# The search for a row's 408th smallest value: counts by paired sums and by signs, settling put between the masks, low halves taken from clamped values

## The chip, the cores and the metric

One core of a Trainium2 chip. TensorE (PE, with its weight loads PEld), VectorE (DVE), ScalarE (ACT), GpSimd (POOL) and SyncE (SP, which starts most DMAs) run programs of their own and meet at semaphores. SBUF and PSUM (eight banks of 512 fp32 columns) have 128 partitions. The metric is the device time of one execution of the whole program, in microseconds, as the median of several runs.

## The reference, cut to what matters

The program is a hybrid of two layers with eight stages over 2048 tokens of 128 channels. The change lies in the first one, an attention of 16 heads whose scores are reduced by a running sum FF and pruned:

```
S = relu(att[:, 0]); S[..., 0] = 0; S = S * (1 - eye(T))
FF = cumsum(S shifted down by one row, axis=1)
att = att - FF[:, None]
memory_budget = int(2048 * 0.2)                  # 409
FF_mod = where(causal, FF, inf)
rank = argsort(argsort(FF_mod, axis=-1), axis=-1)
keep = (rank < minimum(memory_budget - 1, i + 1)) | eye(T)   # 408 smallest of each row
att = where(keep, att, -inf);  y = softmax(att) @ v;  y @ w_proj.T + b_proj
```

Instead of sorting, the kernel finds, for each row with more than 408 allowed columns, the value of its 408th smallest FF, and the attention behind it compares with that threshold. FF is never negative, so an fp32's bits order it as an integer does.

## The kernel before, in words

The 2048 rows are 16 tiles of 128; tile t has rows 128t to 128t+127 on the partitions and W = 128(t+1) columns, held as fp32 in `NF[t]`. Tiles 0 to 2 keep everything; tiles 3 to 15 are searched. Before the search, `take_high` (L835) stores the upper 16 bits (sign cleared) of each value in `halves[t]`, as uint16.

The search (L861 to L933) settles the threshold bit by bit, from the top, for all 128 rows of a tile at once: NC = 32 rounds, k = 0 to 31. Rounds 0 to 14 work on the high halves, 16 to 31 on the low ones. In one round, for each of 13 tiles:

- DVE writes a mask in bf16 (L893, L899): 1 where the half lies below the value found so far plus the bit tried. The masks go round seven buffers (`tally`).
- PE adds up the mask (L923): matmuls with an identity `IDB` accumulate pieces of 256 columns into one bank of PSUM, so 256 partial counts remain. Eight banks go round. A piece with 128 columns is left over for even t.
- ACT reads the 256 columns with `accum_out` (L933), which leaves the count in a column of `cnt`. The accumulator is read out by an instruction of its own, which the compiler adds.
- DVE settles: one instruction compares the counts with `lim` (L879), one adds the bit where the count is low enough (L881).

The tiles form two sets, [15, 12, 11, 8, 7, 4, 3] and [14, 13, 10, 9, 6, 5]. A set is settled as a whole behind all masks of the other set: while DVE writes the masks of one set, PE and ACT finish the counts of the other. The order on each engine is that of the loops in the code; no planner is at work in this stage.

Round 15, the sixteenth, is different. DVE counts the values whose high half lies above the one found (L895) and replaces each half by the lower half of the value where the high half matches and by zero elsewhere (L896), one instruction of scalar_tensor_tensor over the whole tile. `lim` is corrected by that count (L875).

At the end DVE joins the halves into `thr` (L906 to L909), and the attention starts (L1195 on): its first matmuls wait for the last count. Its order was planned ahead (`TileOrder`) and does not depend on times at run time. The DMAs that load the keys for it run beside the search, from 98 to about 172 us.

Of the kernel before, what the change touches and what calls it, by code (L numbers as in the profile page):

```python
# [19 lines left out]
KEEP = 408  # L20
# [368 lines left out]
def build(nc, a, out, stages):  # L389
    ctx = ExitStack()  # L390
    with ctx:
# [12 lines left out]
        def reg(at, n):  # L404
            return A[:, at:at + n]
# [163 lines left out]
        def stage1():  # L569
            NF = [reg(D0 + 64 * t * (t + 1), 128 * (t + 1)) for t in range(NT)]  # L570
            AT = D0 + 17408
# [145 lines left out]
            junk = [reg(2048 + 128 * i, 128).bitcast(BF16) for i in range(8)]  # L717
            IDB = SM[:, 400:464].bitcast(BF16)
# [133 lines left out]
            counts = [(k, i, t) for k in range(NC) for i in range(2) for t in sets[i]]  # L852
            count_no = {x: n for n, x in enumerate(counts)}

            def edges(i):
                return place[sets[i][0]], place[sets[i][-1]] + 1

            def settle_no(k, i):
                return 2 * (2 * k + i + 1)

            def search_vector(e, w):  # L861
                for r in (high, low):
                    e.memset(r, 0.0).then_inc(built, 1)
                e.memset(lim, float(KEEP - 1) + 0.5).then_inc(built, 1)
                w.wait_ge(d_const, 16)
                e.tensor_copy(IDB, IDN).then_inc(built, 1)
                w.wait_ge(built, 4)
                w.wait_ge(f_high, 13)
                w.wait_ge(f_summed, upto[15])

                def settle(k, i):
                    lo, hi = edges(i)
                    w.wait_ge(counted, count_no[k, i, sets[i][-1]] + 1)
                    if k == 15:
                        e.tensor_tensor(lim[:, lo:hi], lim[:, lo:hi], cnt[:, lo:hi], ALU.add).then_inc(settled, 2)  # L875
                        return
                    w.wait_ge(settled, settle_no(k, i) - 2)
                    value, bit = (high, 14 - k) if k < 15 else (low, 31 - k)
                    e.tensor_tensor(hit[:, lo:hi], cnt[:, lo:hi], lim[:, lo:hi], ALU.is_le).then_inc(settled, 1)  # L879
                    w.wait_ge(settled, settle_no(k, i) - 1)  # L880
                    e.scalar_tensor_tensor(value[:, lo:hi], hit[:, lo:hi], float(1 << bit), value[:, lo:hi], ALU.mult, ALU.add).then_inc(settled, 1)  # L881

                for k in range(NC):
                    for i in range(2):
                        if k:
                            w.wait_ge(settled, settle_no(k - 1, i))
                        for t in sets[i]:
                            n, s = count_no[k, i, t], place[t]
                            if n >= 7:
                                w.wait_ge(folded, n - 6)  # L890
                            mask = tally[n % 7][:, 0:128 * (t + 1)]
                            if k < 15:
                                e.tensor_scalar(mask, halves[t], high[:, s:s + 1], float(1 << (14 - k)), ALU.subtract, ALU.is_lt).then_inc(masks, 1)  # L893
                            elif k == 15:
                                e.tensor_scalar(mask, halves[t], high[:, s:s + 1], 0.5, ALU.subtract, ALU.is_gt).then_inc(masks, 1)  # L895
                                e.scalar_tensor_tensor(halves[t], halves[t], high[:, s:s + 1], NF[t].bitcast(U16)[:, 0::2], ALU.is_equal, ALU.mult).then_inc(built, 1)  # L896
                            else:
                                w.wait_ge(built, 4 + 13)
                                e.tensor_scalar(mask, halves[t], low[:, s:s + 1], float(1 << (31 - k)), ALU.subtract, ALU.is_lt).then_inc(masks, 1)  # L899
# [4 lines left out]
                settle(NC - 1, 1)  # L904
                w.wait_ge(settled, settle_no(NC - 1, 1))
                e.tensor_scalar(highi, high, 65536.0, None, ALU.mult).then_inc(built, 1)  # L906
                e.tensor_copy(lowi, low).then_inc(built, 1)
                w.wait_ge(built, 4 + 13 + 2)
                e.tensor_tensor(thr.bitcast(I32), highi, lowi, ALU.bitwise_or).then_inc(built, 1)  # L909
                w.wait_ge(built, 4 + 13 + 3)  # L910

            def search_tensor(e, w):
                w.wait_ge(built, 4)
                w.wait_ge(f_relu, upto[15])
                w.wait_ge(f_copied, upto[15])
                for n, (k, i, t) in enumerate(counts):
                    W = 128 * (t + 1)
                    w.wait_ge(masks, n + 1)
                    if n >= 8:
                        w.wait_ge(counted, n - 7)  # L920
                    for c0 in range(0, W, 256):
                        c1 = min(c0 + 256, W)
                        m = e.matmul(bank(n % 8, c1 - c0), IDB, tally[n % 7][:, c0:c1], start=(c0 == 0), stop=(c1 == W))  # L923
                    m.then_inc(folded, 1)

            def search_scalar(e, w):
                w.wait_ge(part, 10)
                for n, (k, i, t) in enumerate(counts):
                    s = place[t]
                    w.wait_ge(folded, n + 1)  # L930
                    if n >= 8:
                        w.wait_ge(counted, n - 7)
                    e.activation(junk[n % 8], bank(n % 8, 256), ACT.Copy, accum_out=cnt[:, s:s + 1]).then_inc(counted, 1)  # L933

# [1937 lines left out]
```

## Time and profile before

| | us |
|---|---|
| median of 3 runs | 2950.25 (2947.14 to 2955.3) |
| the profiled execution | 2931.04 |
| its span | 2929.3 |
| first mask of the search, on DVE | 98.06 |
| last settling ended | 348.3 |
| mean granted TensorE clock | 0.944 of full speed |

The profile shows one execution; its times are from the start of the span. A group's mean is that of one instruction; instructions of one engine can overlap, so starts are often closer together than the durations say. The profiled execution took 19.2 us less than the median of the timed runs.

### The profile page before, as it was taken

How to read it: one execution, taken by the hardware profiler on the slowest of the kernel's cores; microseconds unless marked ns; L12 is line 12 of the kernel's file. 1: busy time of each engine (PE TensorE's matmuls, PEld its weight loads, DVE VectorE, ACT ScalarE, POOL GpSimd, SP SyncE). 2: the span in 40 equal slices, each digit the busy share in tenths (PEclk: the TensorE clock that was granted, in tenths of full speed). 3: DMA queues.
4: the chain of work that ended last, by engine and by line, in shares of the span. 5: the costliest groups of instructions: out<-in, count | busy, mean ns of one | idle time of the engine just before them, and what ended most of it. 6: DMA issues, size and time to landing. Idle time of an engine off the chain costs nothing. (4 is left out here: it accounts for less than half of the span.)

```text
span 2929.3 us, 75687 instructions
## 1 busy us (share of the span) xinstructions
PE 2600.9 (89%) x31004; PEld 1627.1 (56%) x31004; DVE 1844.5 (63%) x5181; ACT 1783.4 (61%) x3488; POOL 345.6 (12%) x718
## 2 busy tenths in 40 slices
PE   8999878888889799999998989999999999896596
PEld 3677756666666452212213546676676767665355
DVE  6999887887886662100002757877777787663862
ACT  3676655565666338999996246666666667531331
POOL 2100142222221010000000100000000000026026
PEclk7998989999999899999998999999999999898598
DMA  3410010111100202100000010000000000303003
GB/s 117 69 27 2 2 17 17 18 17 17 17 11 3 53 1 91 58 19 1 1 1 17 1 40 7 2 7 7 3 7 7 7 2 2 98 14 49 29 15 58
DMA packets 85120, 68.23 MB, mean 23 GB/s; under 512 B 40776, under 2 KB 73688, under 8 KB 84392
## 3 DMA queue, kind: packets, MB, share of 16 engines
q1 hardware_dynamic: 76328, 57.09, 8.3%
q0 software_dynamic: 8448, 6.30, 1.7%
q8 instruction: 247, 4.05, 0.6%
q14 instruction: 97, 0.79, 0.1%
HBM read 47.21 MB, written 19.96 MB: 23 GB/s over the span
## 5 line engine op out<-in xcount | busy, mean ns | idle before, releaser
L1769 ACT ACTIVATE arena<-ps 128x1024 f32<-128x1024 f32 x512 | 474.1, 1282 | 25.9 <-PE ps L1719 24.0
L1220 DVE CUSTOM_DVE_ANT_0 arena<-ps,arena 128x1024 f32<-128x1024 f32 (+7 forms) x384 | 350.0, 931 | 105.0 <-PE ps L1096 88.5
L2147 DVE CUSTOM_DVE_ANT_0 arena<-ps,arena 128x512 f32<-128x512 f32 (+3 forms) x640 | 371.2, 643 | 26.7 <-PE ps L2011 25.8
L1172 ACT ACTIVATE arena<-ps 128x1024 f32<-128x1024 f32 (+3 forms) x320 | 275.0, 896 | 129.1 <-PE ps L1129 125.7
L2104 ACT ACTIVATE arena<-arena 128x1152 f32<-128x1152 f32 (+15 forms) x256 | 306.4, 1199 | 63.2 <-DVE arena L2147 63.2
L2011 PE MATMUL ps<-arena 64*128 64x512 f32 (+3 forms) x1280 | 270.3, 547 | 3.5 <-ACT arena L2080 1.1
L1730 PE MATMUL ps<-arena 128*32 128x512 f32 x2048 | 273.0, 604 | 0.0
L2042 PE MATMUL ps<-arena 128*64 128x128 f32 x4352 | 262.3, 275 | 0.0
L2042 PEld LDWEIGHTS ps<-arena 128*64 128x64 f32 x4352 | 235.3, 137 | 33.4 <-issue 28.7
L923 PE MATMUL ps<-arena 128*128 128x256 bf16 (+1 forms) x2176 | 238.1, 273 | 13.7 <-DVE arena L895 9.2
L2066 ACT COPY arena<-ps 128x512 f32<-128x512 f32 (+3 forms) x410 | 189.6, 517 | 75.8 <-PE ps L2028 73.6
L1860 DVE COPY arena<-ps 128x512 f32<-128x512 f32 x16 | 11.1, 692 | 356.5 <-PE ps L1730 356.5
L1124 PE MATMUL ps<-arena 64*128 64x64 f32 x4352 | 216.2, 231 | 20.3 <-ACT arena L1172 12.2
L923 PEld LDWEIGHTS ps<-arena 128*128 128x128 bf16 x2176 | 207.5, 99 | 44.9 <-DVE arena L895 13.9
L1719 PE MATMUL ps<-arena 64*128 64x512 bf16 (+1 forms) x1152 | 207.2, 442 | 23.0
L1124 PEld LDWEIGHTS ps<-arena 64*128 64x128 f32 x4352 | 192.9, 144 | 57.7 <-ACT arena L1172 29.2
L1719 PEld LDWEIGHTS ps<-arena 64*128 64x128 bf16 (+1 forms) x1152 | 53.3, 113 | 292.7 <-ACT arena L1769 267.1
L933 ACT ACTIVATE arena<-ps 128x256 bf16<-128x256 f32 x416 | 158.0, 383 | 68.4 <-PE ps L923 58.4
L2028 PE MATMUL ps<-arena 64*128 64x64 f32 x4352 | 178.9, 225 | 11.5 <-DVE arena L2162 3.2
L2011 PEld LDWEIGHTS ps<-arena 64*128 64x128 f32 x1280 | 115.8, 186 | 126.4 <-DVE arena L2147 55.7
L2028 PEld LDWEIGHTS ps<-arena 64*128 64x128 f32 x4352 | 160.6, 139 | 35.0 <-ACT arena L2104 11.9
L2068 DVE COPY arena<-ps 128x512 f32<-128x512 f32 (+3 forms) x230 | 136.4, 622 | 68.8 <-PE ps L2028 67.3
(301 smaller groups left out, 4026.4 us busy)
## 6 DMA issues: line engine op xcount, KB each, us to landing
arena<-scr_q SPq DMA_DIRECT2D x256, 32.0 KB
scr_s<-scr_f SPq DMA_DIRECT2D x1, 4096.0 KB, 16.5
arena<-scr_k SPq DMA_DIRECT2D x32, 128.0 KB
arena<-by_head_k SPq DMA_DIRECT2D x16, 192.0 KB
arena<-scr_s SPq DMA_DIRECT2D x16, 192.0 KB, 2.6
arena<-by_head_q SPq DMA_DIRECT2D x28, 96.0 KB
by_head_k<-arena SPq DMA_DIRECT2D x5, 512.0 KB, 4.5
scr_x<-arena SPq DMA_DIRECT2D x2, 1024.0 KB, 5.2
```

What stands on the lines that cost most here:

```text
L923: m = e.matmul(bank(n % 8, c1 - c0), IDB, tally[n % 7][:, c0:c1], start=(c0 == 0), stop=(c1 == W))
L1124: e.matmul(bank(b + half, 64, 64 * (nb * g + x)), scored_block(u, g)[q, at:at + 128], IDN[q, q], is_transpose=True, start=(g == 0 and x == ...
L1172: e.activation(turned_block(u, kc), src, ACT.Exp, scale=-1.0).then_inc(exped, 1)
L1220: e.tensor_tensor_reduce(scored_block(u, g)[:, lo:hi], PS[:, 1024 * (k % 2):1024 * (k % 2) + hi - lo], NF[t][:, lo:hi], -1.0, mxs[:, col - ...
L1719: m = e.matmul(PS[:, at(n) + 512 * i:at(n) + 512 * i + 512], x, y, start=True, stop=True)
L1730: m = e.matmul(PS[32 * g:32 * g + 32, 3072 + 512 * c:3072 + 512 * c + 512], vp4[:, kt, 4 * g + units[u][0], :], PTR[(2 * s[1] + g // 2) % ...
L1769: e.activation(PTR[k % RS], PS[:, at(n):at(n) + 1024], ACT.Sigmoid, scale=float(1 / np.sqrt(8.0))).then_inc(weighed, 1)
L2011: e.matmul(PS[:, base(step) + 512 * g:base(step) + 512 * g + hi - lo], QA[64 * g:64 * g + 64, 128 * t:128 * t + 128], KA[64 * g:64 * g + 6 ...
L2028: m = e.transpose(PS[:, o:o + 64], block[rows, 512 * kc + 128 * b:512 * kc + 128 * b + 128], IDN[rows, rows])
L2042: m = e.matmul(bank(6 + u % 2, 128)[64 * g:64 * g + 64, :], V[:, 1024 * kt + 64 * h:1024 * kt + 64 * h + 64], halves(plan.ring[u, kc])[:, ...
L2104: e.activation(block, block, ACT.Exp, bias=mxs[:, col:col + 1], scale=-1.0, accum_out=sums(u)[:, g:g + 1]).then_inc(exped, 1)
L2147: e.tensor_tensor_reduce(slot(u, t, g)[:, lo:hi], PS[:, base(step) + 512 * g:base(step) + 512 * g + hi - lo], bias, -1.0, mxs[:, col - 1:c ...
```

## The change

All of it lies in the search and its buffers. Nothing behind `thr` is touched.

- Tiles 3, 4, 5 and 6 get no mask and no matmul. ACT counts them by itself: the Sign of (edge - half) over the tile with `accum_out`, written into a scratch buffer. `edge` is a column that DVE prepares after each settling (`next_edge`).
- The tiles 15 and 8, 12 and 11, 14 and 9, 13 and 10 are summed in pairs into one bank. The mask of the first is multiplied by an identity scaled by 2048 (`IDP`), and ACT reads the bank with Identity and a bias column of 32768, whose 256 additions put the unit of the fp32 sum at one. Both counts then lie in the bits of one number. DVE takes the lower one out (`unpack`) before it compares. Tile 7 has a bank of its own. So there are nine masks, five sums and four signs a round, where there were thirteen masks and thirteen sums.
- A set is settled in four dependent steps (unpack, compare, raise_value, next_edge). They stand between the masks of the other set, one ahead of each from the fourth on, and the rest behind the last mask. After round 14 `bounds` takes the place of `next_edge`: it computes, per row, the smallest and the largest fp32 with the high half found.
- Round 15 counts nothing. DVE clamps each tile's fp32 values to those two bounds (max, then min), into pieces of the `tally` buffers, and the lower halves of the clamped values are copied to `halves`: by ACT for tiles 15, 12, 11, 8, 14, 13, 10, 9, by DVE for 7, 4, 3, 6, 5. `lim` is no longer corrected.
- DVE writes eleven more columns and constants ahead of the first mask.

```diff
-            sets = [[15, 12, 11, 8, 7, 4, 3], [14, 13, 10, 9, 6, 5]]
-            searched = sets[0] + sets[1]
+            ones_of, packs_of = [[8, 11], [9, 10]], [[15, 12], [14, 13]]
+            single_of, direct_of = [[7], []], [[4, 3], [6, 5]]
+            sums_of = [[(packs_of[i][x], ones_of[i][x]) for x in range(2)] + [(t,) for t in single_of[i]] for i in range(2)]
+            masked_of = [[t for x in sums_of[i] for t in x] for i in range(2)]
+            drawn_of = {"act": [15, 12, 11, 8, 14, 13, 10, 9], "dve": [7, 4, 3, 6, 5]}
+            turns_of = [[("clamp", 15), ("clamp", 7), ("clamp", 12), ("draw", 7), ("clamp", 4), ("clamp", 11), ("draw", 4), ("clamp", 3), ("clamp", 8), ("draw", 3)],
+                        [("clamp", 14), ("clamp", 6), ("clamp", 13), ("draw", 6), ("clamp", 5), ("clamp", 10), ("draw", 5), ("clamp", 9)]]
...
+            UNIT, PACK, ALL = 8388608.0, 2048.0, KEEP - 1
+            slots_of = {"act": [(2, 3), (0, 1)] * 4, "dve": [(4,), (6,), (4,), (6,), (4,)]}
+            rounds = [k for k in range(NC) if k != 15]
+            reads = {0: [("sign", 4), ("sum", 0), ("sign", 3), ("sum", 1), ("sum", 2)], 1: [("sign", 6), ("sum", 0), ("sign", 5), ("sum", 1)]}
...
             def search_vector(e, w):
                 for r in (high, low):
                     e.memset(r, 0.0).then_inc(built, 1)
-                e.memset(lim, float(KEEP - 1) + 0.5).then_inc(built, 1)
+                e.memset(spread, UNIT / 256).then_inc(built, 1)
+                e.memset(edge, float(1 << 14) - 0.5).then_inc(built, 1)
...
+                e.tensor_scalar(IDP, IDN, PACK, None, ALU.mult).then_inc(built, 1)
...
+                def unpack(k, i):
+                    ones, packs, _, _ = columns_of(i)
+                    for x in reads[i]:
+                        w.wait_ge(counted, count_no[(k, i) + x] + 1)
+                    e.tensor_scalar(cnt.bitcast(I32)[:, ones], cnt.bitcast(I32)[:, packs], 0x7FF, 0x4B000000, ALU.bitwise_and, ALU.bitwise_or).then_inc(settled, 1)
+
+                def compare(k, i):
...
+                    e.tensor_tensor(hit[:, every], cnt[:, every], lim[:, every], ALU.is_le).then_inc(settled, 1)
+
+                def raise_value(k, i):
...
+                def next_edge(k, i):
...
+                    w.wait_ge(settled, settled_no(k, i, 3))
+                    e.tensor_scalar(edge[:, direct], value[:, direct], step, None, ALU.add).then_inc(settled, 1)
...
-                            elif k == 15:
-                                e.tensor_scalar(mask, halves[t], high[:, s:s + 1], 0.5, ALU.subtract, ALU.is_gt).then_inc(masks, 1)
-                                e.scalar_tensor_tensor(halves[t], halves[t], high[:, s:s + 1], NF[t].bitcast(U16)[:, 0::2], ALU.is_equal, ALU.mult).then_inc(built, 1)
...
+                def clamp(i, t):
...
+                    e.tensor_scalar(clamped_at(t), NF[t], highi.bitcast(F32)[:, s:s + 1], topi.bitcast(F32)[:, s:s + 1], ALU.max, ALU.min).then_inc(built, 1)
+
+                def draw(i, t):
+                    w.wait_ge(built, turned_no["clamp", t])
+                    e.tensor_scalar(halves[t], clamped_at(t).bitcast(U16)[:, 0::2], 0xFFFF, None, ALU.bitwise_and).then_inc(built, 1)
...
-                        if i:
-                            settle(k, 0)
-                        elif k:
-                            settle(k - 1, 1)
+                for k, i, todo in work:
+                    steps = []
+                    if last is not None and last[0] != 15:
+                        steps = [(f,) + last for f in ((unpack, compare, raise_value, bounds) if last[0] == 14 else (unpack, compare, raise_value, next_edge))]
+                    for n, (f, *x) in enumerate(todo):
+                        if n >= 3 and steps:
+                            steps[0][0](*steps.pop(0)[1:])
+                        f(*x)
+                    for f, *x in steps:
+                        f(*x)
+                    last = (k, i)
...
             def search_tensor(e, w):
...
+                for g, (k, i, x) in enumerate(groups):
+                    if g >= 8:
+                        w.wait_ge(counted, count_no[groups[g - 8][0:2] + ("sum", groups[g - 8][2])] + 1)
+                    for t in sums_of[i][x]:
+                        n, W = mask_no[k, i, t], 128 * (t + 1)
+                        w.wait_ge(masks, n + 1)
+                        for c0 in range(0, W, 256):
+                            c1 = min(c0 + 256, W)
+                            m = e.matmul(bank(g % 8, c1 - c0), IDP if t in packs_of[i] else IDB, tally[n % 7][:, c0:c1],
+                                         start=(t == sums_of[i][x][0] and c0 == 0), stop=(t == sums_of[i][x][-1] and c1 == W))
+                        m.then_inc(folded, 1)
...
             def search_scalar(e, w):
...
-                    e.activation(junk[n % 8], bank(n % 8, 256), ACT.Copy, accum_out=cnt[:, s:s + 1]).then_inc(counted, 1)
...
+                        e.copy(halves[t], clamped_at(t).bitcast(U16)[:, 0::2]).then_inc(counted, 1)
...
+                        e.activation(junk[len(read) % 4], bank(g % 8, 256), ACT.Identity, bias=spread, accum_out=cnt[:, s:s + 1]).then_inc(counted, 1)
...
+                        e.activation(signs[x], halves[x], ACT.Sign, bias=edge[:, s:s + 1], scale=-1.0, accum_out=cnt[:, s:s + 1]).then_inc(counted, 1)
```

## Rows read from the trace of the kernel before

**Rows 1.** The page, part 1: busy us, share of the span, instructions.
```profile
PE 2600.9 (89%) x31004; PEld 1627.1 (56%) x31004; DVE 1844.5 (63%) x5181; ACT 1783.4 (61%) x3488; POOL 345.6 (12%) x718
```

**Rows 2.** By stretch: PE, PEld, DVE, ACT, POOL busy us (records); granted clock; DMA; GB/s.
```profile
98.00:107.00 9.00, 8.05 (x61) 6.69 (x62) 8.01 (x19) 4.36 (x20) 0.00 (x0) 0.81 0.57 62
107.00:205.00 98.00, 98.00 (x941) 88.31 (x939) 93.37 (x236) 78.99 (x361) 0.00 (x0) 1.00 0.38 50
205.00:231.00 26.00, 16.32 (x91) 9.12 (x88) 25.84 (x31) 8.52 (x38) 0.00 (x0) 0.63 0.00 1
...
239.00:348.00 109.00, 108.31 (x1038) 97.37 (x1035) 101.18 (x256) 87.85 (x400) 0.00 (x0) 1.00 0.01 2
```

**Rows 3.** Timeline of DVE, one round: start us, us, merged instructions.
```profile
155.34 3.23 DVE L893 TENSOR_SCALAR arena<-arena 128x2048 bf16<-128x2048 uint16 x7
158.49 0.16 DVE L879 TENSOR_TENSOR arena<-arena 128x6 f32<-128x6 f32 x1
158.68 0.17 DVE L881 SCALAR_TENSOR_TENSOR arena<-arena 128x6 f32<-128x6 f32 x1
158.89 2.97 DVE L893 TENSOR_SCALAR arena<-arena 128x1920 bf16<-128x1920 uint16 x6
```

**Rows 4.** Timeline of DVE, the sixteenth round.
```profile
205.07 0.75 DVE L895 TENSOR_SCALAR arena<-arena 128x2048 bf16<-128x2048 uint16 x1
205.74 2.35 DVE L896 SCALAR_TENSOR_TENSOR arena<-arena 128x2048 uint16<-128x2048 uint16 x1
...
230.72 3.23 DVE L899 TENSOR_SCALAR arena<-arena 128x2048 bf16<-128x2048 uint16 x7
```

**Rows 5.** Groups of the search: busy us, mean ns | idle before, releaser.
```profile
L923 PE MATMUL ps<-arena 128*128 128x256 bf16 x1984 | 237.6, 278 | 13.7 <-DVE arena L895 9.2 <-DVE arena L893 3.4 <-DVE arena L899 1.0
...
L933 ACT ACTIVATE arena<-ps 128x256 bf16<-128x256 f32 x416 | 158.0, 383 | 68.4 <-PE ps L923 58.4
...
L893 DVE TENSOR_SCALAR arena<-arena 128x2048 bf16<-128x2048 uint16 x15 | 11.3, 754 | 0.8 <-DVE arena L881 0.3
...
L893 DVE TENSOR_SCALAR arena<-arena 128x512 bf16<-128x512 uint16 x15 | 5.2, 349 | 0.0
```

**Rows 6.** Timeline of DVE, the search's end.
```profile
347.90 0.17 DVE L879 TENSOR_TENSOR arena<-arena 128x6 f32<-128x6 f32 x1 [2.87 <-ACT arena L933]
...
348.30 0.17 DVE L906 TENSOR_SCALAR arena<-arena 128x16 int32<-128x16 f32 x1
348.38 0.17 DVE L907 CAST arena<-arena 128x16 int32<-128x16 f32 x1
```

**Rows 7.** Timeline of ACT, two readings back to back.
```profile
153.71 0.38 ACT L933 ACTIVATE arena<-ps 128x256 bf16<-128x256 f32 x1
...
154.08 0.38 ACT L933 ACTIVATE arena<-ps 128x256 bf16<-128x256 f32 x1
```

**Rows 8.** Groups of ACT, whole kernel, by shape.
```profile
L777 ACT ACTIVATE arena<-ps 128x512 f32<-128x512 f32 x28 | 15.1, 597 | 12.7 <-PE ps L757 12.7
...
L1172 ACT ACT_TABLE_LOAD x1 | 1.3, 1283 | 0.0
...
L2701 ACT ACTIVATE arena<-ps,arena 128x512 f32<-128x512 f32 x4 | 2.4, 682 | 0.0
...
L2104 ACT ACTIVATE arena<-arena 128x896 f32<-128x896 f32 x16 | 16.6, 1036 | 0.0
...
L2104 ACT ACTIVATE arena<-arena 128x512 f32<-128x512 f32 x16 | 11.3, 708 | 0.0
```

**Rows 9.** Groups of DVE outside the search, by shape.
```profile
L837 DVE TENSOR_SCALAR arena<-arena 128x2048 uint16<-128x2048 uint16 x1 | 1.2, 1227 | 0.5 <-POOL arena L805 0.5
...
L2729 DVE TENSOR_SCALAR arena<-arena 128x2048 f32<-128x2048 f32 x1 | 1.2, 1227 | 0.6 <-ACT arena L2690 0.6
...
L491 DVE TENSOR_SCALAR arena<-arena 128x128 f32<-128x128 f32 x128 | 35.7, 343 | 1.2
```

**Rows 10.** Timeline of DVE, the search's start.
```profile
98.06 3.23 DVE L893 TENSOR_SCALAR arena<-arena 128x2048 bf16<-128x2048 uint16 x7
```

More of the change, by code:

```diff
@@ L851, in stage1 @@
             NC = 32
-            counts = [(k, i, t) for k in range(NC) for i in range(2) for t in sets[i]]
-            count_no = {x: n for n, x in enumerate(counts)}
[L855 to L859, printed above, removed]
+            UNIT, PACK, ALL = 8388608.0, 2048.0, KEEP - 1
+            spread = SM[:, 624:625]
+            edge, topi = SM[:, 528:544], SM[:, 688:704].bitcast(I32)
@@ new lines, in stage1, with columns_of @@
+            counts = []
+            for k in range(NC):
+                counts += [(k, "draw", t) for t in drawn_of["act"]] if k == 15 else [(k, i) + x for i in range(2) for x in reads[i]]
+            count_no = {x: n for n, x in enumerate(counts)}
+            group_no = {x: n for n, x in enumerate(groups)}
+            SETTLES = {k: 4 if k < 14 or k > 15 else 6 if k == 14 else 0 for k in range(NC)}
+            def columns_of(i):
+                lo, mid = place[ones_of[i][0]], place[packs_of[i][0]]
+                last, hi = place[direct_of[i][0]], place[direct_of[i][-1]] + 1
+                return slice(lo, mid), slice(mid, mid + 2), slice(last, hi), slice(lo, hi)
@@ new lines, in settled_no, with slots_at, wait_drawn @@
+            def settled_no(k, i, step):
+                return sum(2 * SETTLES[x] for x in range(k)) + i * SETTLES[k] + step
+            def slots_at(t):
+                kind = "act" if t in drawn_of["act"] else "dve"
+                n = drawn_of[kind].index(t)
+                return kind, n, slots_of[kind][n]
+            def wait_drawn(w, kind, n):
+                if kind == "act":
+                    w.wait_ge(counted, count_no[15, "draw", drawn_of["act"][n]] + 1)
+                else:
+                    w.wait_ge(built, turned_no["draw", drawn_of["dve"][n]])
@@ L861, in search_vector, with clamped_at @@
+            def clamped_at(t):
+                return reg(3072 if slots_at(t)[2][0] == 6 else AT + 1024 * slots_at(t)[2][0], 128 * (t + 1))
             def search_vector(e, w):
@@ new lines, in clamp @@
+                def clamp(i, t):
+                    s, (kind, n, slots) = place[t], slots_at(t)
+                    w.wait_ge(settled, settled_no(14, i, 6))
+                    w.wait_ge(folded, max(mask_no[x] for x in masks_order if x[0] < 15 and mask_no[x] % 7 in slots) + 1)
+                    before = [x for x in range(n) if set(slots_of[kind][x]) & set(slots)]
+                    if before:
+                        wait_drawn(w, kind, before[-1])
+                    e.tensor_scalar(clamped_at(t), NF[t], highi.bitcast(F32)[:, s:s + 1], topi.bitcast(F32)[:, s:s + 1], ALU.max, ALU.min).then_inc(built, 1)
@@ new lines, in search_vector @@
+                work = [(k, i, [(mask, k, i, t) for t in masked_of[i]] if k != 15 else [(clamp if kind == "clamp" else draw, i, t) for kind, t in turns_of[i]]) for k in range(NC) for i in range(2)]
+                last = None
+                for k, i, todo in work:
[9 more added lines that the diff above has]
+                    last = (k, i)
@@ new lines, in search_vector @@
+                for f in (unpack, compare, raise_value):
+                    f(*last)
+                w.wait_ge(settled, settled_no(NC - 1, 1, 3))
+                e.tensor_copy(lowi, low).then_inc(built, 1)
+                w.wait_ge(built, N_BUILT + N_TURNS + 1)
+                e.tensor_tensor(thr.bitcast(I32)[:, 0:13], highi[:, 0:13], lowi[:, 0:13], ALU.bitwise_or).then_inc(built, 1)
+                w.wait_ge(built, N_BUILT + N_TURNS + 2)
+            N_BUILT = 4 + 2 * 2 + 4 + 1 + 2
+            turned_no = {x: N_BUILT + n + 1 for n, x in enumerate(turns_of[0] + turns_of[1])}
@@ L912, in search_tensor @@
+            N_TURNS = len(turned_no)
             def search_tensor(e, w):
-                w.wait_ge(built, 4)
+                w.wait_ge(built, N_BUILT)
                 w.wait_ge(f_relu, upto[15])
                 w.wait_ge(f_copied, upto[15])
[L916 to L924, printed above, removed]
+                for g, (k, i, x) in enumerate(groups):
[9 more added lines that the diff above has]
+                        m.then_inc(folded, 1)
@@ L926, in search_scalar @@
             def search_scalar(e, w):
                 w.wait_ge(part, 10)
[L928 to L932, printed above, removed]
-                    e.activation(junk[n % 8], bank(n % 8, 256), ACT.Copy, accum_out=cnt[:, s:s + 1]).then_inc(counted, 1)
+                w.wait_ge(built, N_BUILT)
+                w.wait_ge(f_high, 13)
+                read, signed = [], {0: [], 1: []}
```

101 lines of the change are left out of this document (68 added, 33 removed).

## The prediction

> **What bounds the kernel now.** I read the busy shares first, then a table by stretch, the groups of the search, the timelines of single rounds, and at last rows of other stages that show the operations the change brings in.
>
> The diff touches only the search of the first attention. [rows 1] say nothing about that: PE is busy 89% of the span, but that is an average over eight stages. In [rows 2] the search shows itself, from 98 us to 348 us, in 32 rounds. In the rounds before the sixteenth (107 to 205) PE is busy for all of the 98 us at a granted clock of 1.00, DVE for 93.37, ACT for 78.99. Rounds 17 to 32 look the same. In between, from 205 to 231, DVE has no gap and PE's clock falls to 0.63.
>
> A round is the distance between two starts of the mask of tile 15: 155.34 us [rows 3] and, seven rounds later, 205.07 us [rows 4]: 49.73 / 7 = 7.10 us. PE adds 128(t+1) columns for each of 13 tiles, 16,640 in all; 7.10 us is 0.427 ns a column, one column in a cycle of 2.4 GHz (0.417) and a little for the six tiles with a 128-column remainder. So PE is the first bound, at its peak. DVE is a close second: a mask of W columns takes 0.264 ns x W + 0.21 us by the 2048- and 512-column rows [rows 5], but next starts come sooner: the seven masks of set 0 (8,576 columns) would last 3.73 us and take 3.15 us from 155.34 to 158.49 [rows 3], so 0.083 us of each is overlapped. A settling operation that waits for the one before costs 0.20 us (158.49, 158.68, 158.89). All thirteen make (7.12 - 13 x 0.083) + 4 x 0.20 = 6.84 us a round, and the rest is waiting for counts. A gain therefore needs both engines to lose work, and the change takes it from both.
>
> **Round, PE.** Tiles 3, 4, 5, 6 go to ScalarE: 2,816 columns less, 13,824 left. That pairs share a bank changes no column. 7.10 x 13,824 / 16,640 = 5.90 us.
>
> **Round, DVE.** Nine masks of 1,024 to 2,048 columns: 13,824 x 0.264 + 9 x (0.21 - 0.083) = 4.79 us. Eight small operations instead of four. Where one follows a thing it does not depend on, it starts about 0.08 to 0.10 us after it (348.30, 348.38 in [rows 6]); where it depends, 0.20. Behind set 0's masks: unpack and compare each lie between masks (0.10 each), raise to edge 0.20, edge to the next mask 0.10, so 0.50. In set 1 compare comes after the last mask, so 0.60. Sum 5.89 us. Bounds: eight at 0.08 give 5.4, eight at 0.20 give 6.4 (6.45 with a short wait).
>
> **Round, ACT.** A reading of a bank costs 0.375 us from start to start (153.71 to 154.08, [rows 7]). It becomes Identity with a bias column; 512 columns with such a column last 682 ns against 597 without [rows 8], so +0.085: 5 x 0.46 = 2.30. A Sign over 512 to 896 SBUF columns with bias and accumulation is nearest to the Exp rows of the same sizes, 708 and 1036 ns [rows 8]; 640 and 768 between them by the line, 0.82 and 0.93: 3.49 us. Sum 5.8 us. Bounds: 9 x 0.09 less if the bias column were free and overlapped, 5.0; 0.10 more on each of nine, 6.7.
>
> Three engines thus stand at 5.90, 5.89 and 5.8, and the question is whether the order lets them run side by side. I walk one round, DVE starting mask 15 at 0, with 0.2 us for a hop from engine to engine (an estimate, from the 0.20 between dependent operations) and 0.5 from a reading's start to its count. Mask 15 is usable at 0.8; PE ends set 0 (7,424 columns, 3.15 us) at 3.9; its last sum is seen by ACT at 4.1 and by DVE at 4.65. DVE ends set 0's masks and the settling of set 1 at 3.1 and its third mask of set 1 at 4.75: unpack waits for nothing. PE goes on with set 1 (6,400 columns, 2.75 us) to 6.65; ACT reads Sign 6 to 5.5, bank to 6.0, Sign 5 to 6.9, the last bank to 7.4; DVE wants it at 5.95 + 1.65 = 7.6. Sign 4 of the next round fills 7.4 to 8.2, and its first bank is ready at 8.3. It closes, with 0.1 to 0.2 us to spare. This is what the edit "behind the third mask" costs: the margin before was the whole set. I take 6.05 us. The ends for the main case are 5.90 (PE) and 6.45 (DVE with every small operation at 0.20). Per round 1.05 us; 31 rounds (the sixteenth is gone as a search round): 32.6 us.
>
> **Round sixteen.** Before: 205.07 to 230.72 [rows 4], 25.65 us, of which the multiply-and-select (2.35 us for 2,048 columns, so by columns 19 us for all) is the most. After: 13 clamps and 5 draws on DVE, 8 draws on ACT. A clamp is fp32 with two columns as scalars. The fp32 row without them is 1227 ns for 2,048, 0.52 ns a column [rows 9]; the 128-column row with two is 343 ns, so 0.28 + 0.52 x 0.128. Start to start 0.19 + 0.52 ns x W: 16,640 x 0.52 + 13 x 0.19 = 11.1 us. The five draws read every second half-word, as the take of the high halves does (1227 ns for 2,048, [rows 9]): 3,840 x 0.52 + 5 x 0.08 = 2.4. Six settling operations of round 15 lie inside (0.9), and the first half of round 17 has none (-0.5). Sum 13.9 us. ACT's eight draws (12,800 x 0.85 + 8 x 0.15 = 12.1) run beside, each one clamp late; the two ring slots never stop DVE by this count, and the mask of tile 15 waits for the draw of tile 10, at 14.7 less 0.5. I take 14.2, a gain of 11.4 us. Bounds: if clamps go 1.04 ns a column, +8.7; if ACT hides wholly and the fixed costs are half, -1.5.
>
> **Start, restarts, tail.** Eleven more small writes ahead of the first mask (98.06, [rows 10]), on the path: 0.6 us (0 to 1.5). PE starts cold twice, at 98 and at 231 (0.81 and 0.63 in [rows 2]); before, that cost 0.5 us (15 rounds from 98.06 to 205.07, less 15 x 7.10) and 0.7 us (16 rounds from 230.72 to 347.90, less 16 x 7.10 and the tail), since PE's lag was covered by a whole set. With the shorter margin I take 1.4 each, +1.6 together (0 to 4). Tail: DVE stands 2.87 us before the last settling [rows 6], since PE lags behind; PE now lags less (7.4 + 0.1 against the round's 6.05): -1.3, one more dependent step +0.2.
>
> **Sum.** -32.6 - 11.4 + 0.6 + 1.6 - 1.1 = -42.9 us. After the search nothing changes, and it starts on the end of the search, so all of it is passed on. The profiled execution took 2931.04 us around its span of 2929.3; it becomes 2888. The timed median lies 19 us above the profiled time; the difference is taken from the median: 2950.25 - 42.9 = 2907.
>
> **A rule that speaks against the change.** [rows 5, 8] show 349 ns for DVE's mask of 512 columns and 708 ns for an activation of that size. The Trainium skill, in "ScalarE: Activation LUTs", "Rules for kernel authors", says to give simple elementwise work to VectorE and not to ScalarE, up to about 3x faster in bf16. The trace agrees with the price. It would leave all thirteen masks on DVE, and the round at 7.10. Here ACT had 19 of 98 us free of any reading, and readings fall from thirteen to five, so the dearer place is the cheaper one until ACT's sum passes PE's, which by the numbers above is 0.1 us away.
>
> **Rivals.**
> *ACT is the bound.* For it: 5.8 us in order, margins of 0.1 to 0.2. Against: the Exp rows already hold bias and accumulation. With 0.10 more on each of nine the round is 6.7, +20 us: 2927; halfway 2917. Chance 0.15.
> *Clamps at one element a cycle.* For it: 343 ns is also 0.21 + 1.04 x 0.128, and 0.21 is the mask's fixed part. Against: one scalar column costs 60 ns over none (mask 754 less 0.26 x 2,048 is 0.22; the row without has 0.16), a second brings 0.28, which fits the fast form. +8.7: 2916. Chance 0.12.
> *Table switches, slower than before.* If Sign and the bank readings needed different tables, ScalarE would load one at each of the eight changes between them in a round: 8 x 1.283 us [rows 8] on top of 5.8 gives 16.1 us a round, +10 x 31 = +311 against the main case: 3218. It decides from a round of 7.45 us on, that is 1.3 loads. For it: Exp behind a copy brings a load at the end of the search. Against: the search's Copy, Relu and the Sqrt before run with none between them. Chance 0.02.
> The Trainium skill, "ScalarE: Activation LUTs", "Table sets", names relu, copy, identity and abs as filler of every set and not Sign in that sentence, and prices a switch at 2.7 us; by it the rival would cost twice as much, or nothing if Sign is filler too.
> *The gain given back* (PE's clock falls since it no longer has a full queue): in 205 to 231 PE is busy 16.3 of 26 us at 0.63 [rows 2]. At 1.2 GHz a round is 11.8 us, which is slower than before. With PE 5.9 of 6.05 busy it is unlikely: 0.02. A mild form that ends within 0.3% of before: 0.02.
>
> **How the numbers follow.** Forecast 0.67, the others as given. The forecast's own range is 2899 to 2914. The two middle rivals stretch it upward; 5.90 a round and a quick sixteenth end at 2950.25 - 49 = 2901, with a spread of some 4 us in the runs themselves 2896. Range 2896 to 2926. Changes under 0.3% (9 us) can't be told from none here. Faster 0.94, same 0.02, slower 0.04.
>
> **What would show it.** In the after profile: rounds of 6.05 us by starts of tile 15's mask; PE idle a little in each and its clock at 1.00; the unpack waiting under 0.1 us for ACT (more means the ACT rival); no table load between 98 and 305 us; a clamp of 2,048 columns at 1.35 us (2.3 means the clamp rival); about 14 us between rounds 15 and 17; the search ending near 305 us. The forecast is wrong if the round is over 6.45 us.

## The result, and the profile after

| | before | after |
|---|---|---|
| median of 4 runs, us | 2951.44 (2947.14 to 2955.3) | 2907.73 (2902.26 to 2911.71) |
| ratio | | 0.985 (95%: 0.9834 to 0.9866) |
| profiled execution, its span | 2931.04, 2929.3 | 2907.81, 2906.0 |
| search: first mask to the attention's first instruction on VectorE | 98.06 to 348.80: 250.7 | 97.16 to 307.81: 210.6 |
| a steady round | 7.10 | 6.02 |
| from tile 15's mask in round fifteen to that in round seventeen | 7.10 + 25.65 | 20.53 |
| the first round, and the first behind round sixteen | 7.56, 7.79 | 8.55, 8.75 |

The kernel is 43.7 us faster; 42.9 were forecast. The profiled spans differ by 23 us only, because two later stages were some 20 us shorter in the trace of before, which has nothing to do with the change (below). One execution of the kernel unpaired (below) took 10,745 us and is in none of the figures.

The table by stretch of the kernel after, to be read against [rows 2] (the same columns). Outside the two restarts PE and ACT are both near full; in [rows 2] ACT had a fifth of its time free.

```profile
98.00:107.00 9.00, 8.94 (x61) 7.09 (x62) 5.79 (x15) 4.89 (x17) 0.00 (x0) 0.71 0.57 59
107.00:191.00 84.00, 82.65 (x771) 72.15 (x769) 79.54 (x234) 81.14 (x247) 0.00 (x0) 1.00 0.42 57
191.00:206.00 15.00, 1.35 (x13) 1.01 (x11) 14.72 (x31) 13.02 (x16) 0.00 (x0) 0.65 0.00 1
206.00:214.00 8.00, 7.17 (x43) 5.46 (x44) 4.66 (x10) 4.83 (x12) 0.00 (x0) 0.59 0.00 0
214.00:300.00 86.00, 86.00 (x802) 75.10 (x800) 82.86 (x244) 84.63 (x258) 0.00 (x0) 1.00 0.01 2
```

One round on VectorE's timeline, against [rows 3] (start us, us, operation): unpack (L928), compare (L933), raise (L939), edge (L946). Compare starts 0.08 us before the mask ahead of it ends (187.28 + 0.61 against 187.81), as masks do among themselves. Unpack starts 0.06 us after the end of its (185.40 + 1.74 against 187.20; 188.55 + 1.77 against 190.37). These 0.14 us, twice a round, are waiting, though too short for a bracket.

```profile
185.40 1.74 DVE L982 TENSOR_SCALAR arena<-arena 128x2048 bf16<-128x2048 uint16 x3
187.20 0.17 DVE L928 TENSOR_SCALAR arena<-arena 128x2 int32<-128x2 int32 x1
187.28 0.61 DVE L982 TENSOR_SCALAR arena<-arena 128x1536 bf16<-128x1536 uint16 x1
187.81 0.16 DVE L933 TENSOR_TENSOR arena<-arena 128x6 f32<-128x6 f32 x1
187.88 0.48 DVE L982 TENSOR_SCALAR arena<-arena 128x1024 bf16<-128x1024 uint16 x1
188.28 0.16 DVE L939 SCALAR_TENSOR_TENSOR arena<-arena 128x6 f32<-128x6 f32 x1
188.48 0.17 DVE L946 TENSOR_SCALAR arena<-arena 128x2 f32<-128x2 f32 x1
188.55 1.77 DVE L982 TENSOR_SCALAR arena<-arena 128x1920 bf16<-128x1920 uint16 x3
190.37 0.17 DVE L928 TENSOR_SCALAR arena<-arena 128x2 int32<-128x2 int32 x1
```

What unpack waits for at 190.37 stands on ACT's timeline: the last bank of set 0, whose accumulator is read out until 190.24. ACT itself had to wait for PE ahead of 189.22 (the Sign before it had been read out at 189.12, the reading behind it follows after 0.47).

```profile
189.22 0.47 ACT L1042 ACTIVATE arena<-ps,arena 128x256 bf16<-128x256 f32 x1
...
189.69 0.47 ACT L1042 ACTIVATE arena<-ps,arena 128x256 bf16<-128x256 f32 x1
190.04 0.20 ACT L1042 ACTIVATION_READ_ACCUMULATOR arena<-ps,arena 128x1 f32 x1
```

The groups of the search, against [rows 5] and the rows of other stages from which they had been estimated, [rows 8, 9]: mean ns of one behind the comma.

```profile
L1042 ACT ACTIVATE arena<-ps,arena 128x256 bf16<-128x256 f32 x155 | 72.5, 469 | 11.6 <-PE ps L1021 8.7
L1053 ACT ACTIVATE arena<-arena 128x896 bf16<-128x896 uint16 x31 | 32.1, 1035 | 0.0
...
L982 DVE TENSOR_SCALAR arena<-arena 128x2048 bf16<-128x2048 uint16 x31 | 23.1, 746 | 0.1
...
L1053 ACT ACTIVATE arena<-arena 128x512 bf16<-128x512 uint16 x31 | 22.0, 710 | 0.0
...
L1034 ACT COPY arena<-arena 128x2048 uint16<-128x2048 uint16 x1 | 1.9, 1898 | 0.0
...
L963 DVE TENSOR_SCALAR arena<-arena 128x2048 f32<-128x2048 f32 x1 | 1.3, 1345 | 0.0
```

Forecast: 0.46 us for a bank's reading (469 ns measured), 1036 and 708 ns for the signs (1035 and 710), 1.35 us for the clamp (1345), 0.85 ns a column and a little for the copy (1898 for 2,048). No table load stands among the groups until the attention's first Exp.

VectorE's first rounds and the end of the search, against [rows 10] and [rows 6]: in the brackets the idle time before.

```profile
97.16 4.36 DVE L982 TENSOR_SCALAR arena<-arena 128x2048 bf16<-128x2048 uint16 x8
104.66 0.17 DVE L928 TENSOR_SCALAR arena<-arena 128x2 int32<-128x2 int32 x1 [3.14 <-ACT arena L1042]
```

```profile
306.78 0.17 DVE L928 TENSOR_SCALAR arena<-arena 128x2 int32<-128x2 int32 x1 [1.34 <-ACT arena L1042]
...
307.60 0.17 DVE L1002 TENSOR_TENSOR arena<-arena 128x13 int32<-128x13 int32 x1
```

Before, VectorE stood 2.87 us ahead of the last settling, now 1.34.

### The profile page after: what moved, and what is told of

Same layout as the page of the kernel before. It is cut to its first block and busy times, and to the rows that moved or that the text cites. A ratio compares the mean times of both kernels' runs of the same rounds, so it can differ in the third digit from the quotient of the medians.

```text
span 2906.0 us, 73996 instructions
## 1 busy us (share of the span) xinstructions
PE 2553.9 (88%) x30564; PEld 1586.3 (55%) x30564; DVE 1802.5 (62%) x5184; ACT 1796.3 (62%) x3222; POOL 347.1 (12%) x718
## 5 line engine op out<-in xcount | busy, mean ns | idle before, releaser
L1981 DVE COPY arena<-ps 128x512 f32<-128x512 f32 x16 | 11.1, 692 | 356.5 <-PE ps L1851 356.5
L1021 PE MATMUL ps<-arena 128*128 128x256 bf16 x1736 | 192.0, 273 | 19.6 <-DVE arena L982 18.3
L1021 PEld LDWEIGHTS ps<-arena 128*128 128x128 bf16 x1736 | 165.9, 99 | 46.3 <-ACT arena L1034 14.7
L1263 PE MATMUL ps<-arena 128*32 128x128 f32 x4352 | 164.6, 278 | 1.4 <-ACT arena L1293 1.3
```

Of the source, the lines that this page charges most:

```text
L1021: m = e.matmul(bank(g % 8, c1 - c0), IDP if t in packs_of[i] else IDB, tally[n % 7][:, c0:c1], start=(t == sums_of[i][x][0] and c0 == 0), ...
```

## The experiments

Each is a change to the kernel after. Times of whole kernels are compared only within a comparison on one chip; the round and the search are read from the traces, where steady rounds repeat to 0.01 us (in pool_edge and six_masked they scatter over 0.06, and the mean stands here).

| | first, k = 0 | steady round | over round sixteen, mask to mask | first behind it | search | ratio to before |
|---|---|---|---|---|---|---|
| after | 8.55 | 6.02 | 20.53 | 8.75 | 210.6 | 0.985 |
| after_again | 8.89 | 6.02 | 20.54 | 8.00 | 208.7 | 0.9855 (0.983 to 0.9881) |
| after_third | 8.85 | 6.02 | 20.53 | 7.96 | 208.7 | 0.9842 (0.9821 to 0.9863) |
| warm | 8.86 | 6.02 | 20.52 | 5.95 | 206.8 | 0.9848 (0.9818 to 0.9879) |
| settle_last | 8.56 | 6.12 | 21.15 | 8.56 | 212.3 | 0.9857 (0.9823 to 0.989) |
| pool_edge | 8.52 | 5.98 | 20.58 | 7.92 | 207.6 | 0.9846 (0.9815 to 0.9876) |
| draws_vector | 7.30 | 6.02 | 27.54 | 8.71 | 215.1 | 0.9883 (0.9838 to 0.9927) |
| unpaired | 8.77 | 7.54 | 22.04 | 7.63 | 253.3 | 1.001 (0.9991 to 1.0029) |
| six_masked | 9.05 | 6.34 | 21.72 | 8.84 | 220.4 | 0.990 (0.9853 to 0.9946) |
| warm_both | 6.02 | 6.02 | 20.52 | 5.95 | 203.7 | 0.9821 (0.9803 to 0.9839) |

**The two kernels again.** No edit.

> The changed kernel once more, for a second trace and a tighter interval. Theory: the search again takes 6.02 us a round by starts of tile 15's mask, 14.2 us for round sixteen, 8.5 us for each first round after a cold start, and the 17 us between what the search gained (40 to 41 us) and what the two profiled spans differ by (23.3 us) lie in stages 6 and 8 as scatter from execution to execution, so the timed ratio stays near 0.985 and stage 6 and 8 take another length here. Rival: the change itself makes stages 6 and 8 longer; then this trace shows the same 10 us more in each as the first one after the change.

> The kernel before once more, for a second trace. Its first trace had 223.7 us from the start of stage 6's routing to that of stage 8's and 154.1 from there to the end; four traces with the change have 234 to 237 and 164 to 167. Theory (the first trace was a quick one in stages 6 and 8): here the two lengths are about 234 and 164 and the span is near 2950 us; the search takes 250.7 us again. Rival (the change makes stages 6 and 8 longer by 20 us): here they are 224 and 154 again.

The search repeats in both. Stages 6 and 8, the two with indirect DMAs, decide the rest: from the activation of stage 6's routing to that of stage 8's, and from there to the end, it was 223.7 and 154.1 us in the first trace of before, 234.1 and 163.8 in the first of after, 234.6 and 166.0 in after_again. In before_again it was 222.7 and 153.5, not near 234 and 164 but as the rival had it. The rival's cause fails even so: in after_third, on the chip of a later comparison where before has a median of 2930.03 us, the kernel after has 224.3 and 152.8. So the changed kernel has both lengths, and the change does not make the stages longer. (The kernel before has been traced in the short form alone; that its timed runs of 2951 and 2956 us had the long one is inferred.) Every trace with the change from the comparisons with before at 2951 and 2956 us has the long form, every trace from those with 2929 and 2930 the short one. What makes it so is left open.

**warm.** PE is kept at work while VectorE clamps and draws.

```diff
+                    if (k, i, x) == (16, 0, 0):
+                        for turn in range(N_TURNS):
+                            w.wait_ge(built, N_BUILT + turn + 1)
+                            for _ in range(7):
+                                e.matmul(bank(g % 8, 128), IDB, IDB, start=True, stop=True)
```

> PE issues 7 small matmuls of the identity on itself after each of the 18 clamps and draws of round sixteen, into the bank that the next sum overwrites. Theory (the half clock costs the restart): the granted clock is 1.00 when the masks come back, the first round after it falls from 8.6 us to about 6.5, and the whole is 2 us faster; the first round at 97 us stays at 8.5. Rival (refilling the pipeline from mask to count costs it): the first round stays at 8.5 us whatever the clock.

The table by stretch, round sixteen and the 8 us behind it, first of after_again, then of warm (PE, PEld, DVE, ACT, POOL, granted clock):

```profile
191.00:205.00 14.00, 0.26 (x3) 0.03 (x1) 13.86 (x25) 12.03 (x12) 0.00 (x0) 0.68 0.00 0
205.00:213.00 8.00, 7.26 (x50) 5.78 (x51) 5.33 (x14) 5.47 (x15) 0.00 (x0) 0.70 0.00 0
```

```profile
191.00:205.00 14.00, 10.24 (x130) 7.59 (x130) 13.86 (x27) 12.08 (x9) 0.00 (x0) 1.00 0.01 2
205.00:213.00 8.00, 8.00 (x78) 7.07 (x76) 7.29 (x21) 7.43 (x25) 0.00 (x0) 1.00 0.00 0
```

With 10.24 of 14 us busy PE keeps a granted clock of 1.00, and the round behind takes 5.95 us instead of 8.00 or 8.75. Kept at work, PE has no restart to pay: refilling from mask to count costs nothing that can be seen. The search is 1.9 us shorter than in after_again, and the median 1.6 us lower, which two executions can't tell from none.

That it is the clock can be read from the other traces too. Behind round sixteen of the first trace of after it stood at 0.50, and then at 1.00:

```profile
207.00:212.00 5.00, 5.00 (x26) 3.63 (x25) 3.29 (x7) 2.21 (x7) 0.00 (x0) 0.50 0.00 0
213.00:220.00 7.00, 7.00 (x69) 6.16 (x67) 6.15 (x19) 6.90 (x21) 0.00 (x0) 1.00 0.00 0
```

In every kernel with rounds of 6.02 us a restart cost half of the time for which PE, back at work, was held at 0.50, to about 0.1 us: 2.65 us at 0.50 cost 1.28 (draws_vector, the start), 4.10 cost 1.99 (after_again, behind round sixteen), 5.19 cost 2.53 and 5.65 cost 2.73 (after), 5.93 cost 2.87 (after_again, the start). So the scatter of the first rounds in the table is the scatter of that time.

**warm_both.** The same, and ahead of the first mask:

```diff
+                for _ in range(16):
+                    e.matmul(bank(0, 128), IDN, IDN, start=True, stop=True)
```

> The changed kernel, to be set beside warm_both on the same chip. Theory: ratio to before 0.985 as in the other comparisons, rounds of 6.02 us, first rounds of 8.5 to 8.9 us at 97 us and of 8.0 to 8.8 at 206 us.

> The matmuls of warm in round sixteen, and 16 fp32 matmuls of the identity more between the last matmul of the running sums and the first mask. Theory (the half clock at both starts costs the first rounds): both first rounds about 6.0 to 6.2 us, the granted clock 1.00 from 94 us on, the whole 4.5 to 5 us faster than the changed kernel, a ratio to it of 0.998, which five rounds may just tell. Rival (the first round is long at 97 us since ScalarE and the banks are filled for the first time, or since the key loads take the memory): it stays over 8 us.

By stretch in warm_both (columns as above): at a clock of 1.00 all through, the first round takes 6.02 us.

```profile
94.00:98.00 4.00, 3.78 (x35) 3.46 (x35) 3.96 (x21) 0.93 (x3) 0.00 (x0) 1.00 0.57 61
98.00:106.00 8.00, 8.00 (x78) 7.01 (x76) 7.21 (x21) 7.80 (x25) 0.00 (x0) 1.00 0.58 72
...
190.00:204.00 14.00, 10.94 (x134) 8.47 (x134) 13.86 (x26) 11.60 (x14) 0.00 (x0) 1.00 0.00 1
204.00:212.00 8.00, 8.00 (x77) 7.06 (x75) 7.20 (x22) 7.90 (x25) 0.00 (x0) 1.00 0.00 0
```

The search falls to 203.7 us, 5.0 less than in after_third on the same chip, and the medians are 2877.95 (2875.41 to 2882.2) and 2883.65 us (2879.38 to 2890.74): 5.7 us apart. The ranges overlap, so the time alone says only that it is likely; the traces say where it comes from. This version has the shortest search and the lowest ratio of those that were run.

**settle_last.**

```diff
-                        if n >= 3 and steps:
+                        if n >= 99 and steps:
```

> All four settling steps behind the last mask of the other set, as before the change, all else as changed. Theory (VectorE's own sequence sets the round, with all waits covered): only overlaps between small operations are lost, one dependent step of 0.1 us more in set 0 and one in set 1, so 6.22 us a round, +6 us in all, but the cold restarts get cheaper, 7.5 instead of 8.5 us, since the margin is larger; net +4 us. Rival (counts arrive late and the early settling costs waits): the round is not longer than 6.02.

VectorE's timeline, one set: the steps now follow each other at 0.20 us.

```profile
152.62 0.17 DVE L928 TENSOR_SCALAR arena<-arena 128x2 int32<-128x2 int32 x1
152.83 0.17 DVE L933 TENSOR_TENSOR arena<-arena 128x7 f32<-128x7 f32 x1
153.03 0.17 DVE L939 SCALAR_TENSOR_TENSOR arena<-arena 128x7 f32<-128x7 f32 x1
153.23 0.17 DVE L946 TENSOR_SCALAR arena<-arena 128x2 f32<-128x2 f32 x1
153.31 2.67 DVE L982 TENSOR_SCALAR arena<-arena 128x2048 bf16<-128x2048 uint16 x5
```

The round is 6.12, so it grows by half of what was expected. Here unpack starts before the last mask's end (150.44 + 2.27 against 152.62) and waits for nothing: 6.12 us is VectorE's own sequence. In the kernel after the sequence is shorter, but unpack is 0.14 us late in each set, so part of the early settling's gain is given back as waiting. The first rounds are no shorter (8.56 and 8.56), but here PE was held at 0.50 for 6.00 us at both restarts, of which half is 3.00, and they cost 8.56 - 6.12 = 2.44 each. So the later settling does cover 0.56 us of a restart, where about 1 us was expected. Settling early is worth 31 x 0.10 = 3 us.

**pool_edge.** `next_edge` is taken from VectorE's steps and stands in a loop on GpSimd, which waits for raise.

```diff
-        (unpack, compare, raise_value, next_edge)
+        (unpack, compare, raise_value)
+            def search_gpsimd(e, w):
+                for k, i in edges_order:
...
+                    w.wait_ge(settled, settled_no(k, i, 3))
+                    e.tensor_scalar(edge[:, direct], value[:, direct], step, None, ALU.add).then_inc(filled, 1)
```

> The edge for the signs is made by GpSimd instead of VectorE, twice a round. Theory (VectorE bounds at 6.02, with TensorE at 5.90 and ScalarE at 5.90 busy behind it): VectorE's sequence falls by 0.2 us a set to 5.6, the round to 5.95, between PE's 5.90 and ACT's busy time with its gaps, 2 to 3 us less in all. Rival 1 (ACT is already the bound): the round stays at 6.02 and VectorE now waits for ACT at unpack. Rival 2 (the hop over GpSimd is late): ACT waits for GpSimd before a Sign and the round is longer than 6.02.

VectorE's timeline (raise and the masks behind it), GpSimd's, and the groups of the two masks beside which GpSimd works:

```profile
150.47 0.16 DVE L941 SCALAR_TENSOR_TENSOR arena<-arena 128x6 f32<-128x6 f32 x1
150.66 1.83 DVE L977 TENSOR_SCALAR arena<-arena 128x1920 bf16<-128x1920 uint16 x3
```

```profile
150.71 0.22 POOL L1010 TENSOR_SCALAR arena<-arena 128x2 f32<-128x2 f32 x1 [2.94 <-DVE arena L941]
```

```profile
L977 DVE TENSOR_SCALAR arena<-arena 128x2048 bf16<-128x2048 uint16 x13 | 10.3, 795 | 0.5
L977 DVE TENSOR_SCALAR arena<-arena 128x1920 bf16<-128x1920 uint16 x13 | 10.0, 768 | 0.5
```

The round is 5.95 to 6.01, 5.98 in the mean, where 5.95 was expected, and the search 207.6 us, 1.1 less than in after_again and not 2 to 3. Two things eat the 0.2 us a set. The edge cost VectorE only 0.08 us, because the mask behind raise waits for raise itself (150.47 to 150.66, 0.19 us) while it started 0.08 us behind the edge. And the masks that run beside GpSimd's operation take 795 and 768 ns against 746 and 712 in the kernel after, 0.1 us a round. ACT waits for no edge, and VectorE waits for ACT once between 108 and 180 us, so neither rival came.

**draws_vector.** The turns are 13 clamps and 13 draws, with one or two turns between a clamp and its draw, in buffers of `tally` in turn.

```diff
-            drawn_of = {"act": [15, 12, 11, 8, 14, 13, 10, 9], "dve": [7, 4, 3, 6, 5]}
+            drawn_of = {"act": [], "dve": [15, 12, 7, 11, 4, 8, 3, 14, 13, 6, 10, 5, 9]}
```

> All 13 draws of low halves on VectorE, none on ScalarE. Theory (VectorE sets the length of round sixteen): 12,800 columns more at 0.52 ns and 8 x 0.08 us, 7.3 us; round sixteen 14.2 + 7.3 = 21.5 us, mask to mask 27.8 us instead of 20.5, the rounds of 6.02 unchanged. Rival (it would wait for ScalarE's draws anyhow, so the copies there only hide): less than 5 us more.

```profile
184.35 1.74 DVE L984 TENSOR_SCALAR arena<-arena 128x2048 bf16<-128x2048 uint16 x3
...
211.89 1.74 DVE L984 TENSOR_SCALAR arena<-arena 128x2048 bf16<-128x2048 uint16 x3
```

From mask to mask (first and last line of that stretch of VectorE's timeline) 27.54 us against 20.53: 7.0 more, where 7.3 were expected. ScalarE's eight copies are hidden but for 0.11 us in the kernel after, for which its first mask behind them waits.

**unpaired.**

```diff
-            sums_of = [[(packs_of[i][x], ones_of[i][x]) for x in range(2)] + [(t,) for t in single_of[i]] for i in range(2)]
+            sums_of = [[(15,), (8,), (12,), (11,), (7,)], [(14,), (9,), (13,), (10,)]]
-                    e.tensor_scalar(cnt.bitcast(I32)[:, ones], ...
+                    e.tensor_scalar(SM[:, 704 + 2 * i:706 + 2 * i].bitcast(I32), ...
```

> Nine sums of one tile each, signs kept; unpack writes to an unused column, so that VectorE's work is the same. TensorE's columns are the same too. Theory (the pairs are there for ScalarE): ACT has 9 x 0.465 + 3.49 = 7.7 us a round and becomes the bound: round 7.7 to 7.9 us against 7.10 before the change, 31 x 1.75 = +54 us over the changed kernel, so the whole is at or above the kernel before. Rival (ScalarE has slack that the busy time hides): under 7.0 us a round.

One round by stretch (7.50 us, then PE, PEld, DVE, ACT): ACT is full, the others are not.

```profile
130.00:137.50 7.50, 6.50 (x58) 5.08 (x56) 5.75 (x18) 7.50 (x27) 0.00 (x0) 1.00 0.57 92
```

The round is 7.54 us and the kernel is as slow as before: 2931.4 us against 2929.02. Signs without pairs would have brought nothing at all. Pairs without signs were not run; that they alone would leave the round at 7.10 us is argued from TensorE's columns and VectorE's masks, which they do not change.

**six_masked.**

```diff
-            single_of, direct_of = [[7], []], [[4, 3], [6, 5]]
+            single_of, direct_of = [[7], [6]], [[4, 3], [5]]
```

> Tile 6 is masked and summed again instead of signed. Theory (VectorE's sequence is the bound): one mask of 896 columns more, 0.448 - 0.083 = 0.36 us: 6.38 us a round, +11 us in all. Rival 1 (TensorE is the bound): 896 columns by 0.427 ns more on 5.90 gives 6.28. Rival 2 (ScalarE is the bound, 5.8 of 6.02): it loses 1.04 and gains 0.465, so the round gets shorter than 6.02.

The waits from 108 to 180 us (who, for whom, us in total, times, longest): VectorE's unpack waits in each of the twelve rounds, and ACT waits for PE.

```profile
ACT arena L1042 <- PE ps L1021: 9.4, 11, 0.9
DVE arena L928 <- ACT arena L1042: 2.6, 12, 0.2
```

6.34 us. It rules out ACT's busy time as the bound, and by itself lies between the two others: ACT waits for PE, and VectorE for ACT, so it is not VectorE's sequence alone either. The starts of the matmuls tell more: one follows the other at its columns' pace all round, but for 0.06 us ahead of the first one of tile 14. PE's 6.28 us and that wait make 6.34.

## Why the prediction was right, step by step

- **The rounds.** Forecast 6.05, measured 6.02: 31 x 1.08 = 33.5 us where 32.6 stood. It held in ScalarE's terms: 469 ns for a reading, 710 to 1035 for the signs. Two smaller things cancelled. VectorE's sequence without waits is 6.02 less 2 x 0.14, 5.74 us and not 5.89. And the walk through the round said that unpack waits for nothing, with 0.1 to 0.2 us to spare; it comes 0.14 us late in each set. That step failed, by 0.2 to 0.3 us a set. The text gave a wait of over 0.1 us there as the sign of ScalarE being the bound; it was the sign of the loop below.
- **What sets the round.** The text had three engines near 5.9 and left it open. The timelines show a loop over all three: mask 15 starts at 185.40 and can be used about 0.75 us later; PE sums 15, 8, 12 and 11 (6,400 columns, 2.73 us at the 0.427 ns of the rounds before); ACT reads that bank from 189.22, 0.34 us behind; unpack comes 1.15 us later, at 190.37; then a mask, compare, raise and edge, and mask 15 of the next round 1.05 us later (111.66 after 110.61, where no sixteenth round is in the way). 0.75 + 2.73 + 0.34 + 1.15 + 1.05 = 6.02 us. At each hand-over the one who takes has to wait: PE 0.12 us for mask 15 (its matmuls start at 186.11 and 186.29, elsewhere 0.06 us behind one of 128 columns), ACT 0.10 us ahead of 189.22, VectorE 0.14 ahead of 190.37. PE's wait is the only one in its round, so the round is also PE's 5.90 us, as forecast, and 0.12 for the hand-over. It fits pool_edge by size: 0.08 us less behind raise, 0.05 more for mask 15. settle_last is out of the loop and stands on VectorE alone, 0.1 us longer; PE idles 0.22 us a round there. The loop is argued from starts, waits and sizes; no run takes one of its links away. Of the rivals, ACT as the bound did not come, but it was near: ScalarE idles 0.10 us in a round.
- **The early settling.** There is no slack for a stall. In the first trace of after, PE's queue stopped 1.35 us at 124.85 us, waiting for nothing that the profile shows, and unpack waited 1.56 us one set later; that round took 7.53 us. In four other traces (after_again, after_third, warm, draws_vector) PE's queue stops near the same place for 0.08 to 0.14 us, and that round takes 6.10 to 6.15: each stop is passed on whole. (So is the long one: by the starts of the matmuls it is 1.51 us.) In settle_last a stop of 0.14 us leaves the round at 6.12, so there it is covered. What stops the queue is open. Both lines of the long stop (idle before in brackets):

```profile
126.20 1.03 PE L1021 MATMUL ps<-arena 128*128 128x256 bf16 x8 [1.35 <-issue]
```

```profile
130.17 0.17 DVE L928 TENSOR_SCALAR arena<-arena 128x2 int32<-128x2 int32 x1 [1.56 <-ACT arena L1042]
```

- **Round sixteen.** Forecast 14.2, measured 20.53 less 6.02, which is 14.5, in which `bounds` took 0.3 us more than `next_edge` would have. Clamps went in the fast form; the rival at one element a cycle did not come. draws_vector confirms that VectorE sets its length and that the copies on ScalarE hide but for 0.1 us.
- **The restarts, the one term that was too small.** The text put 0.9 us more on each than before (1.4 in place of 0.5). They cost 8.55 - 6.02 = 2.5 and 8.75 - 6.02 = 2.7 in the first trace, 2.9 and 2.0 in after_again, where before had 0.5 and 0.7: about +4 us, not +1.6, at the end of the stated 0 to 4. warm and warm_both show why. The forecast took the cost of before and added 0.9 us for the shorter margin; in fact the loop has no margin, and half of the time at the granted clock of 0.50 (5.19 and 5.65 us in the first trace) is lost whole. In before it was at 0.50 for 3.41 and 4.04 us of PE's work and the first rounds grew by 0.5 and 0.7 only, since VectorE ran further ahead of PE: from mask 15's start to its first matmul it is 0.90 us in the first round of before and 2.1 from the second on, but 0.8 to 0.9 in every round of after. Whether this spared the kernel before any time, or only put it where the starts of masks don't show it, no run tells.
- **Start and tail.** The eleven writes took about 0.3 us of the 0.6 (96.54 to 97.16 us, where those of the kernel before took 97.78 to 98.06). The wait ahead of the last settling fell by 1.5 where 1.3 was forecast; from the last mask of tile 15 to the attention, less a round, it is 0.9 us less, where 1.1 was forecast.
- **The sum.** Search 250.7 to 210.6 is -40.1 in the first trace, -41.6 between the repeated ones (250.3 and 208.7), against -42.9, or -43.5 without the writes ahead of the search. The measured terms close it: -33.5 for the rounds, -11.1 for round sixteen, +4.0 for the restarts and -0.9 for the tail make -41.5, and the stop of the queue adds 1.5 in the first trace. So the forecast was near because the rounds were right; of the restarts' miss of 2.4 us, 0.9 was made good by rounds a little shorter than forecast, which was luck. The timed differences are 43.7, 42.2 and 46.4 us in three comparisons, within their intervals of each other.
- **The difference from the median.** The prediction took the gain from the timed median and not from the profiled execution. That was luck in so far as nothing had shown why they differed by 19 us; the traces now have stages 6 and 8 differing by some 10 us each from one comparison to the next.
- **Tables.** No load came, so Sign went with what ScalarE had active. The Trainium skill, "ScalarE: Activation LUTs", "Table sets", holds that cheap functions are in every set, and does not name Sign among them; in this trace Sign went like one of them, in the one set that was active.

## What to carry to other kernels

Where two engines share a bound, work must leave both, and the third that takes it must first be relieved: the signs paid only because the paired sums had freed ScalarE (7.54 against 6.02 us a round). A price taken from a row of the same shape in another stage, with its bias column and accumulator, was right to 2%, though it was of another function. A loop over three engines without slack passes every delay on: half of the time at the half clock, and each stop of a queue. Settling late costs 0.1 us a round and covers 0.6 us of a restart; 126 small matmuls beside the clamps and draws and 16 ahead of the search, whose sums nobody reads, took 5 us off, more than the settling's order is worth.

## What the runs showed of the hardware that was not expected

- PE held a granted clock of 1.00 with 10.24 of 14 us busy in matmuls of 128 columns (warm); left idle for 14.5 to 15 us it was at 0.50 when the work came back and rose 4.0 to 6.0 us later (after, after_again, after_third, settle_last, pool_edge).
- A GpSimd operation on two columns (0.22 us) lengthened a VectorE mask beside it by 37 to 56 ns; the masks without one beside them kept their length to 8 ns.
- The same kernel has stages 6 and 8 together 20 us longer in some comparisons than in others (224.3 and 152.8 us in after_third, 234.6 and 166.0 in after_again; the timed kernel before has 2951 to 2956 us in comparisons with the long form and 2929 to 2930 in those with the short); the ratio of the kernels hardly moves.
